# TensorE repeats a product of a matrix of ones while it waits, in a four-layer graph network on one core

## The reference, cut to what matters

```python
h = max(layernorm(x), 0); x = x + attention(h)      # six 1024x1024 products, 16 heads over 384 nodes with a
                                                    # mask scattered from the edges, one output product
h = max(layernorm(x), 0); x = x + rgcn_gated(h)     # root product, 8 relations, gate product of 2048x1024
h = max(layernorm(x), 0); x = x + sage_two_layers(h)
h = max(layernorm(x), 0); x = x + h @ W_sparse.T + bias   # W scattered from 6144 edge weights
```

## Time and profile before

| | us |
|---|---|
| median of 3 runs | 1020.43 (1014.75 to 1021.98) |
| the profiled execution, its device time | 1018.43 |
| its span, first to last instruction | 1016.6 |
| TensorE busy | 941.5 |
| mean granted clock | 0.966 |

### The profile page before, as it was taken

The page is one execution under the profiler, slowest core; times in us unless marked ns, Lnnn a source line. Parts: engine busy times, 40 slices in busy tenths (PEclk is TensorE's granted clock), DMA queues, the critical chain, the costliest instruction groups (busy, mean ns, idle before and its releaser), DMA issues.

```text
span 1016.6 us, 13971 instructions
## 1 busy us (share of the span) xinstructions
PE 941.5 (93%) x4743; PEld 841.1 (83%) x4743; DVE 605.3 (60%) x1043; ACT 367.3 (36%) x575; POOL 484.6 (48%) x409
## 2 busy tenths in 40 slices
PE   2999999994898979999999999999999969999994
PEld 2999999994797977888888888888888848887883
DVE  6888888862897344556455464554556464545625
ACT  5333333331686244322222222222225333334321
POOL 4133334775798443265374664755658203114312
PEclk9999999996999998999999999999999979999997
DMA  8966656531443526444544444444333513323301
GB/s 216 280 208 204 204 157 171 140 63 23 94 93 88 145 63 212 145 104 147 149 119 142 105 156 154 107 141 121 94 111 109 186 63 108 121 103 104 124 21 63
DMA packets 85784, 131.18 MB, mean 129 GB/s; under 512 B 22312, under 2 KB 63464, under 8 KB 85736
## 3 DMA queue, kind: packets, MB, share of 16 engines
q1 hardware_dynamic: 68800, 126.22, 39.6%
q0 software_dynamic: 15360, 0.08, 3.6%
q10 hardware_dynamic: 1576, 4.27, 1.3%
HBM read 116.65 MB, written 7.59 MB: 122 GB/s over the span
## 4 chain that ended last, share of the span: by engine, by line
PE 69%; DMA 18%; DVE 5%; issue 3%; POOL 3%; ACT 2%; ACTq 0%; DVEq 0%; POOLq 0%; SPq 0%
PE ps L571 48%; DMA mask_d<-type_val,cell 12%; PE ps L618 8%; PE ps L443 4%; DMA count_d<-met,cell 4%; PE ps L491 2%; PE ps L515 2%; PE ps L422 1%; PE ps L502 1%; POOL count_d L1446 1%; DVE stats L1015 1%; DMA b_in<-in_L_gnn_bo 1%; PE ps L480 1%; PE ps L722 1%; PE ps L433 1%
## 5 line engine op out<-in xcount | busy, mean ns | idle before, releaser
L1136 DVE TENSOR_TENSOR wlo<-raw,whi 128x1024 fp32r<-128x1024 f32 x120 | 198.2, 1655 | 143.2 <-ACT whi L828 143.1
L443 PE MATMUL ps<-acts,whi 128*128 128x384 f32 (+1 forms) x896 | 229.9, 337 | 4.4 <-DVE acts L1116 4.4
L1485 POOL TENSOR_TENSOR mean_lo<-mean_f,mean_hi 128x384 fp32r<-128x384 f32 x80 | 89.4, 1118 | 189.7 <-ACT mean_hi L927 189.7
L443 PEld LDWEIGHTS ps<-acts,whi 128*128 128x128 f32 x896 | 162.4, 189 | 4.6 <-issue 4.6
L443 PE MATMUL ps<-acts,wlo 128*128 128x384 f32 (+1 forms) x448 | 150.3, 336 | 0.0
L927 ACT ACTIVATE mean_hi<-mean_f 128x384 fp32r<-128x384 f32 x80 | 42.0, 526 | 298.1 <-DVE mean_f L1249 298.1
L571 PE MATMUL ps<-whi,mean_hi 128*128 128x512 f32 x480 | 149.0, 392 | 0.0
L571 PE MATMUL ps<-whi,mean_lo 128*128 128x512 f32 x480 | 147.8, 389 | 0.0
L571 PE MATMUL ps<-wlo,mean_hi 128*128 128x512 f32 x480 | 147.8, 389 | 0.0
L828 ACT ACTIVATE whi<-raw 128x1024 fp32r<-128x1024 f32 x120 | 125.4, 1049 | 22.3 <-PE ps L571 21.7
L571 PEld LDWEIGHTS ps<-wlo,mean_hi 128*128 128x128 f32 x480 | 90.2, 188 | 19.9
(11 more groups left out here) (154 smaller groups left out, 1543.8 us busy)
## 6 DMA issues: line engine op xcount, KB each, us to landing
raw<-in_L_gnn_weight SPq DMA_DIRECT2D x64, 512.0 KB, 3.3
rows_b<-rows_d SPq DMA_DIRECT2D x24, 384.0 KB, 5.1
raw<-in_L_gnn_w_gate SPq DMA_DIRECT2D x16, 512.0 KB, 3.3
raw<-in_L_gnn_W_self SPq DMA_DIRECT2D x16, 512.0 KB, 3.3
raw<-in_L_gnn_W_neigh SPq DMA_DIRECT2D x16, 512.0 KB, 3.3
count_d<-total_r SPq DMA_DIRECT2D x8, 576.0 KB, 4.2
rel_r<-count_d SPq DMA_DIRECT2D x8, 576.0 KB, 4.4
raw<-in_L_gnn_wq SPq DMA_DIRECT2D x32, 128.0 KB, 7.0
```

What stands on the lines that cost most here:

```text
L443: mm = pe.matmul(ps[:, j % 2, 0:N], stationary[j % RING][:, k, :], acts[:, a, moving, k, :], start=i == 0, stop=i == 3 * KT - 1)
L1136: dve.tensor_tensor(wlo_row[slot], raw[slot][:, :], whi_row[slot].bitcast(F32), ALU.subtract)\
L1485: pool.tensor_tensor(mean[1][:, k % 2, :], mean_f[:, k % 2, :], mean[0][:, k % 2, :].bitcast(F32), ALU.subtract).then_inc(S["mean_lo"], 1)
```

## The change

A helper `keep_busy(bank, n)` on TensorE repeats one product, `ones_r` (128x128, fp32r) by `ones_r`, n times into the first 128 columns of a bank that holds nothing needed at that time. It is called: 48 times over after the edge fields are turned; 24 times after `START` is turned; in `begin(0)` 24 times at once and 24 more behind each of two waits on `var_ready`; in `begin(1)` 24 times behind each of two waits on `x_gated`, and 24, 24 and 16 times behind three waits on `var_ready`; before the last layer 24 times and 24 more behind each of two waits on `var_ready`. Together 328 products: 72 in the opening, 72, 112 and 72 in the three layer norms. No other engine's list is touched. The wait on `agg_read` of the last layer moves ahead of the one on `h_ready`.

```diff
             mm.then_inc(S["edges_turned"], 1)
+            def keep_busy(bank, n):
+                for _ in range(n):
+                    pe.matmul(ps[:, bank, 0:P], ones_r[:, :], ones_r[:, :], start=True, stop=True)
+
+            pe.wait_ge(S["ones_made"], 3)
+            keep_busy(1, 48)
             pe.wait_ge(S["bcol_in"], 16 * 7)
             pe.transpose(ps[:, 1, 0:7 * KT], b_in[:, :], ident[0:7 * KT, 0:7 * KT]).then_inc(S["edges_turned"], 1)
...
             pe.wait_ge(S["edge_cols"], 1)
+            keep_busy(0, 24)
             pe.wait_ge(S["bcol_made"], 1)
             pe.wait_ge(S["start_lo"], len(START))
...
                 y0 = (Y_H1, Y_H2, Y_MID)[q]
+                if q == 0:
+                    keep_busy(2, 24)
+                    for seen in (NT + 1, 2 * NT):
+                        pe.wait_ge(S["var_ready"], seen)
+                        keep_busy(2, 24)
+                if q == 1:
+                    for seen in (4, 6):
+                        pe.wait_ge(S["x_gated"], seen)
+                        keep_busy(7, 24)
+                    for nt in range(NT):
+                        pe.wait_ge(S["var_ready"], 2 * NT + nt + 1)
+                        keep_busy(7, 24 if nt < NT - 1 else 16)
                 pe.wait_ge(S["h_ready"], H_FIRST[q + 1])
...
+            pe.wait_ge(S["agg_read"], (KT + 1) * (R + 2))
+            keep_busy(7, 24)
+            for nt in range(1, NT):
+                pe.wait_ge(S["var_ready"], 3 * NT + nt + 1)
+                keep_busy(7, 24)
             pe.wait_ge(S["h_ready"], H_ALL[4])
-            pe.wait_ge(S["agg_read"], (KT + 1) * (R + 2))
```

## The result

The changed kernel takes 1025.41 us (median of 15 runs, 1020.13 to 1036.49), the kernel before 1016.81 us (15 runs, 1012.28 to 1021.98): ratio 1.0074, interval 1.0050 to 1.0098. It is slower by some 7.5 us, inside the 1% I had called no change, but clear of the measurement's interval. The ratio leaves out the longest execution, 1036.49 us, because it lies over 1.5% above the fastest; with it the medians are 8.6 us apart. The profiled execution has a span of 1019.9 us, 3.3 more than the one before, and a mean clock of 0.985 instead of 0.966. So the clock went up and the time too.

The account below looks back on a forecast made before the run. TensorE, busy 941.5 of 1016.6 us, was taken to set the pace. Opening +1.0, layer 2 -1.0, layer 3 +1.1, last norm -1.0 made +0.1 us on 1018.43, put at 1020 for a median; range 1012 to 1032.

Parts of the forecast that it names:

- Price of a product: All bursts: one 128-column fp32r product of ones takes 0.11 us at the high clock, 0.20 at the low.
- the line through 384 and 512 columns: Product price extrapolated from wider products' spacing (0.17 and 0.22 us): 0.066 us at 128 columns if weight loads stay hidden.
- Cheap products: Rival for all bursts: 0.066 to 0.08 us each, -7.6 us in all, 1011 to 1014 us; chance 0.14.
- loads that don't overlap: Rival for all bursts: 0.187 us a product, 234 on the path, +18 us, 1038 us; chance 0.08.
- Layer 2: Norm of layer 2: row block ready 1.8 us later, its 14 products save 2.8 at the high clock; sum -1.0 us.
- Layer 3: Norm of layer 3: row block 3.4 us later, 11 products at the high clock save 2.3; sum +1.1 us.
- Opening: Start of the kernel: clock rises during the 48 products, ACT's copy 2.0 us late, DVE takes some back; put at +1.0 us.
- Last norm: Norm before the last layer: bursts end +0.3 us, transposes save 0.36 and 0.3, last products 0.7; sum -1.0 us.
- thin work was borne there: Untouched norm, 914.0 to 917.3: with only 1.01 us of work in 3.3 us, the clock stayed up.
- the clock isn't raised by them, but held: Rival: products of ones hold a high clock but don't raise it; only the opening pays, +4 us, 1024; chance 0.07.
- not busy enough: Rival: products don't count as work, clock falls in each norm; opening +5.0, last +4.6, in all +28 us, 1046; chance 0.10.
- The ceiling: Whole price at stake: half of 17.8 us of dense work at half clock in four places, 8.9 us or 0.9%.

Follow-up runs that it names:

- the kernel with the opening alone: Only the opening's 48 and 24 products of 128 columns of ones kept, norms idle as before; against the kernel before: ratio 1.0029 (1.0004 to 1.0054).
- the best kernel: Fitted bursts of 384-column products in all three norms, also between and behind the last norm's turned blocks; against the kernel before: ratio 0.9924 (0.9897 to 0.9951).
- the single places: Three kernels keeping only the changed kernel's bursts in the opening, layers 2 and 3, or last norm; against the kernel before: ratios 1.0029, 1.0021, 1.0042.

## Why the prediction was wrong

It said 1020 us, no measurable change; the kernel is 0.74% slower. That 1025.41 lies inside the range it gave is luck: the range stood around a median of three executions of the kernel before, 1020.43, where fifteen give 1016.81.

- **Price of a product**: 0.112 and 0.217 us against 0.11 and 0.20. The argument from the longer fp32r loads held, the line through 384 and 512 columns did not. The 0.20 was a mean: in the 32 transposes it came from the clock rose at 252.6, and up to there they start 0.213 us apart. Cheap products and loads that don't overlap are both out.
- **Layer 2**: -0.9 us against -1.0. **Layer 3**: +1.4 against +1.1 in the profiled execution. The bursts end too late by the same sums, though the near agreement in layer 2 owes something to the one profile before (the spread is 0.9 us). That some executions lose the clock in layer 3 was not foreseen.
- **Opening**: +4.4 us against +1.0. The step that failed is "Dense work needed 3.2 to 5.9 us before the clock rose, mean 4.45. So 4.4 us at 0.20 are 22 products, the other 26 take 2.9 us". It took the products of ones for dense work. All 48 ran at the low clock and `START` came at 20.12, not 17. With wide products in the same place the clock did rise, after 3.1 us. The second sum of that part, that DVE takes back some of the delay, held: of the 6.1 us by which `START` is late 4.4 arrive at the scatter (3.2 to 6.4 by the spread).
- **Last norm**: +6.7 us against -1.0. The step that failed is the clock at the second burst: the sum has it at the high clock from 998.12 to 1000.8, so it let the clock survive the pause of 1.2 us behind a thin burst. Instead 48 products took 10.2 us, the transposes started 14.1 us after the last row block instead of 8.8, and 19 of the last 27 products ran at the low clock instead of 9.
- **The row it leaned on**: "thin work was borne there", in the untouched norm of layer 3, was a draw. In eight of the twelve experiments' profiles the clock fell there for 3.4 us, just behind the turned blocks, and the stretch from the first row block of layer 3 to the last one took 154.4 to 154.6 us instead of 153.0. In the kernel with the opening alone, for example, the turned blocks start at 916.29, and the clock is down in the middle row (same columns as the earlier trace rows):

```profile
916.20:918.60 2.40, 1.46 (x9) 1.14 (x10) 1.02 (x2) 2.36 (x5) 0.00 (x0) 1.00 0.57 179
918.80:922.00 3.20, 3.20 (x9) 2.43 (x8) 1.15 (x1) 0.00 (x0) 0.00 (x0) 0.50 0.32 92
922.20:925.00 2.80, 2.80 (x15) 2.29 (x14) 0.10 (x1) 0.63 (x2) 0.00 (x0) 1.00 0.20 80
```

- **The rivals**: "the clock isn't raised by them, but held" was right in its mechanism for the opening (+4 against +4.4), but I gave it 0.07 and did not carry it to the last norm; "not busy enough" was right there (+4.6 against +6.7) and wrong in layers 2 and 3. I had weighed the two as cases for the whole kernel, where each place has its own. Against "not busy enough" I had set the f32 transposes that brought the clock up; they did, but products of 128 columns did not, so the likeness was the wrong witness. With the opening at +4.4 and the last norm at +6.7 in place of +1.0 and -1.0 the sum of the prediction would have been +11.2 us, near the +11.6 of the touched places and above the 7.5 us timed.
- The ceiling holds within the noise: half of the low-clock time is 8.9 us, of which 7.0 lie in the three norms, and the best kernel, which leaves the opening alone, gives back 7.7 (5.0 to 10.5).

Not settled: why the timed loss is 7.5 us where the touched places of one execution make 11.6, the single places timed +3.0, +2.1 and +4.3, 9.4 in all, each with an interval of 2 us or more to either side. The clock rises and falls at other times in each profile, as the spread above shows, so no single profile stands for the median.

## What to carry to other kernels

Being busy by the profile was not enough here. Products of 384 columns, the width of many of the real ones, brought a low clock up and held a high one over a pause; products of 128 columns never brought it up and did not always hold it over a pause. So take the width of the real products for work that is added only to hold TensorE's clock, unless a run shows that less will do; where the limit between the two widths lies was not measured. Thin products did hold a high clock when nothing but thin work lay between two stretches of real work.

Fill each wait up to its end and not past it, counted by the product's own measured spacing, and leave no gap between the real work and the first burst. Before anything is added, sum what the low clock costs in all (0.9% here), and look what else is waiting: in this opening a scatter that starts after six comparisons, which gained nothing from a faster TensorE and lost with a later one. And look at several profiles before a row of one is taken for how the clock behaves.

## What the hardware showed that I had not expected

- The same engine, busy for 100% of a stretch by the profile, may or may not raise the clock: 48 products of 128 columns in 10.4 us did not (three profiles), 10 of 384 columns in 3.1 us did (one). A thin stream held a high clock for 8 to 12.6 us in five stretches of three profiles.
- A pause beside a thin burst may cost the clock. It was lost behind 1.23 us in the last norm in three profiles of three, behind 0.90 us in layer 3 in one of three, and behind the 1.2 to 1.7 us of the opening in one of three. Behind wide bursts it held over 1.25 and 1.56 us, one profile each.
- The column of the granted clock reads 1.00 until the first change that is recorded, also where 48 products take 0.217 us each; the pace of a known instruction is the better witness.
- Once down, the clock stayed down for 20.5 us in the last norm of the changed kernel (994.9 to 1015.4), through 48 products, 9 transposes and 19 real products.
